# Attention in strips of the tensor array, double-width evictions, and a ring of its own for the residual's input

## What is computed

```python
def xattn(query, key_value, Wq, bq, Wk, bk, Wv, bv, Wo, bo):     # 16 heads of 32
    q, k, v = query @ Wq + bq, key_value @ Wk + bk, key_value @ Wv + bv   # then split into heads
    attn = softmax(clip(einsum('bhqd,bhkd->bhqk', q, k) * 32 ** -0.5, -10000, 10000))
    return einsum('bhqk,bhkd->bqhd', attn, v).reshape(B, Nq, Cq) @ Wo + bo

def ffn(x, emb, w1, w2):                 # 8 experts, each token to its best 2, capacity 1024
    weights = router(x, emb)             # softmax over the two best logits
    # of each expert the first 1024 tokens that chose it
    inter = relu(tokens @ w1[e].T);  out = (inter @ w2[e].T) * gate
    # scattered back by addition

x = x + xattn(layernorm(x), ctx, ...)
x = x + ffn(layernorm(x), ...)
```

## Time and profile before

| what | value |
|---|---|
| time, median of 3 runs | 1538.28 us (1538.25 to 1545.6) |
| time of the profiled execution | 1524.85 us |
| its span, first to last instruction | 1523.1 us |
| mean granted TensorE clock | 0.965 of full speed |
| PE busy | 1411.5 us (93%) |
| DVE busy | 982.1 us (64%) |
| ACT busy | 825.6 us (54%) |
| POOL busy | 857.8 us (56%) |
| DMA | 215.09 MB, 141 GB/s |

### The profile page before, as it was taken

One profiled execution on the slowest core, in us unless ns is written; L12 is line 12 of the kernel. 1 busy time (PEld: TensorE's weight loads), 2 busy tenths in 40 slices (PEclk: granted clock), 3 DMA queues, 4 the chain that ended last, 5 costly groups with the idle time before them and its releaser, 6 DMA issues.

```text
span 1523.1 us, 23892 instructions
## 1 busy us (share of the span) xinstructions
PE 1411.5 (93%) x8807; PEld 875.2 (57%) x8807; DVE 982.1 (64%) x1950; ACT 825.6 (54%) x1472; POOL 857.8 (56%) x907
## 2 busy tenths in 40 slices
PE   6787999989998999999964899999999999999996
PEld 2565777768776777768743644444444444444442
DVE  7895898978877877787766454545454555545430
ACT  4675787668886888768854451504233342425120
POOL 2596788879997899878966414232232414151301
PEclk9898999999999999999976999999999999999998
DMA  6166877568664655746734347465556556474401
GB/s 227 47 154 141 187 200 175 128 143 209 149 145 92 150 122 129 191 102 148 187 93 142 98 129 182 128 171 149 149 164 159 161 127 165 125 196 116 114 14 42
DMA packets 312062, 215.09 MB, mean 141 GB/s; under 512 B 252345, under 2 KB 252729, under 8 KB 311946
## 3 DMA queue, kind: packets, MB, share of 16 engines
q1 hardware_dynamic: 295411, 162.84, 43.6%
q0 software_dynamic: 15360, 50.66, 11.3%
q10 hardware_dynamic: 1175, 0.07, 0.1%
HBM read 105.62 MB, written 50.86 MB: 103 GB/s over the span
## 4 chain that ended last, share of the span: by engine, by line
PE 79%; DVE 5%; SPq 4%; POOL 4%; ACT 3%; issue 2%; DMA 2%; ACTq 1%; DVEq 0%; POOLq 0%
PE ps L1314 22%; PE ps L1335 22%; PE ps L634 9%; PE ps L773 7%; PE ps L752 7%; PE ps L670 5%; SPq L494 3%; PE ps L827 2%; PE ps L601 2%; POOL put L1006 1%; PE ps L796 1%; POOL ph L735 1%; DMA pT<-ph 1%; PE ps L464 1%; DMA wvf<-wv 1%
## 5 line engine op out<-in xcount | busy, mean ns | idle before, releaser
L1314 PE MATMUL ps<-xT,w1s 128*128 128x512 f16 (+1 forms) x1632 | 335.2, 368 | 0.0
L1335 PE MATMUL ps<-w2s,hT 128*128 128x512 f16 x1536 | 332.8, 379 | 0.0
L1320 ACT ACTIVATE hT<-ps 128x512 f16<-128x512 f32 (+1 forms) x136 | 77.8, 572 | 359.7 <-PE ps L1314 359.7
L1314 PEld LDWEIGHTS ps<-xT,w1s 128*128 128x128 f16 x1632 | 160.4, 98 | 172.3
L1335 PEld LDWEIGHTS ps<-w2s,hT 128*128 128x128 f16 x1536 | 150.2, 98 | 181.3
L1345 POOL DMA_INDIRECT out_dram<-ys,idx x64 | 71.7, 1120 | 277.6 <-DVE ys L1340 277.6
L634 PE MATMUL ps<-xnT,wqh 128*128 128x256 f16 x1536 | 189.4, 280 | 9.4 <-DVE xnT L614 7.5
L1322 DVE SCALAR_TENSOR_TENSOR hT<-ps,hT 128x512 f16<-128x512 f32 (+1 forms) x136 | 88.9, 658 | 140.6 <-ACT hT L1320 140.5
L735 POOL TENSOR_TENSOR ph<-sd,ph 128x1232 f16<-128x1232 f32 x64 | 161.9, 2530 | 30.6 <-ACT ph L731 30.5
L634 PEld LDWEIGHTS ps<-xnT,wqh 128*128 128x128 f16 x1536 | 153.6, 101 | 33.1 <-DVE xnT L614 9.0
L752 PE MATMUL ps<-pT,vb 128*128 128x256 f16 (+1 forms) x1248 | 161.5, 278 | 11.6 <-issue 10.3
(11 more groups left out here) (185 smaller groups left out, 2200.3 us busy)
## 6 DMA issues: line engine op xcount, KB each, us to landing
xs<-x SPq DMA_DIRECT2D x64, 256.0 KB, 2.9
xt<-x SPq DMA_DIRECT2D x64, 256.0 KB, 3.1
xrow_dram<-x SPq DMA_DIRECT2D x64, 256.0 KB, 3.3
out_dram<-x SPq DMA_DIRECT2D x64, 256.0 KB, 3.5
stage<-w1T SPq DMA_DIRECT2D x8, 2048.0 KB, 10.1
stage<-w2T SPq DMA_DIRECT2D x8, 2048.0 KB, 8.4
wqf<-wq SPq DMA_DIRECT2D x1, 1024.0 KB, 7.7
wof<-wo SPq DMA_DIRECT2D x1, 1024.0 KB, 11.8
```

Of the source, the lines that this page charges most:

```text
L1314: do("pe", lambda q, k=k, a=a, b=b, i=i, last=last: q.matmul(hb[z][:, 0:wide], w1s[e % 2][:, a, k, ic * P:(ic + 1) * P], xT[:, 4 * b + k, ...
L1335: do("pe", lambda q, k=k, a=a, b=b, i=i, last=last: q.matmul(yb[z][:, :], hT[:, a, k, s * P:(s + 1) * P], w2s[e % 2][:, b, k, :], start=(k ...
```

## The change

Keys and queries of one head share 32 partitions. The change addresses the tensor array by strips.

- `s_mm`: one call per tile. Each head gets a matmul of its own on its 32 rows (row strip j) with 77 columns, 48 per tile; strip j writes bank `bS[j]`, so each bank holds one head of every group. All four banks must be free before a tile's scores, and both maxima wait for all of them.
- The heads' order changes by that, so the value columns (`head_at`) and the output weight's rows (four loads) are permuted.
- `pv_mm`: each head writes its own 32 output partitions (column strip j) with the strip's 32 value columns; a head whose keys lie in two chunks has two pieces: 25 pieces by 3 products, 75 matmuls of 256 columns per pair. Two groups share one bank, 256 columns each; `o_hi` and `o_lo` handle 512 columns, two per pair.
- `part` becomes `partq` (2 x 256) for the queries and `parto` (2 x 512) for the output.
- `xt` is a ring of three, freed by the normalisation. The tile is loaded once more (`load_r`) into `xr`, a ring of five freed by the residual; `add_bo` works on it and waits for the load alone.
- `x1T` has one buffer. Planner's ranks and some costs change.

```diff
-XT = 9
+XT = 3
+RT = 5
...
-    "ln1_stats": -6.54, "rsqrt1": 17.94, "ln1_apply": 18.24, "add_bo": 22.74, "tx": -4.11, "tx_hi": 26.0,
...
+    "ln1_stats": 24.37, "rsqrt1": 19.72, "ln1_apply": 29.94, "add_bo": 34.21, "tx": 7.36, "tx_hi": 37.47,
...
-    "tx_lo": 0.65, "q_mm": 1.4, "q_hi": 0.87, "q_lo": 0.76, "s_mm": 0.42, "s_max": 0.45, "s_sub": 0.9, "s_min": 1.32, "s_exp": 1.32,
+    "tx_lo": 0.65, "q_mm": 1.4, "q_hi": 0.87, "q_lo": 0.76, "s_mm": 0.62, "s_max": 0.45, "s_sub": 0.9, "s_min": 1.32, "s_exp": 1.32,
...
-    "pv_mm": 1.15, "o_hi": 0.78, "o_lo": 0.76, "o_mm": 2.7, "residual": 0.0, "t2": 0.5, "t2_copy": 0.6,
+    "pv_mm": 1.7, "o_hi": 1.2, "o_lo": 1.25, "o_mm": 2.7, "residual": 0.0, "t2": 0.5, "t2_copy": 0.6,
...
+        xr = sb("xr", [P, RT, D], F32)
...
-        part = sb("part", [P, 4, GW], F32)
+        partq = sb("partq", [P, 2, GW], F32)
+        parto = sb("parto", [P, 2, 2 * GW], F32)
...
-        x1T = sb("x1T", [P, 2, 4, P], F32)
+        x1T = sb("x1T", [P, 4, P], F32)
...
         def load_x(t):
             dma("sp", lambda e: e.dma_start(xt[:, t % XT, :], x_t[t]), ("l_x", t), t % XT,
-                after=[("x1", t - XT)] if t >= XT else [])
+                after=[("n1", t - XT)] if t >= XT else [])
+
+        def load_r(t):
+            dma("sp", lambda e: e.dma_start(xr[:, t % RT, :], x_t[t]), ("l_r", t), t % RT,
+                after=[("x1", t - RT)] if t >= RT else [])
...
-        dma("sp", lambda e: e.dma_start(wof[:, :, :], wo.rearrange("(c p) n -> p c n", p=P)), ("l_wo",))
-        for t in range(4, XT):
-            load_x(t)
+        wo_j = wo.rearrange("(j g d) n -> j d g n", j=4, g=4)
+        for j in range(4):
+            dma("sp", lambda e, j=j: e.dma_start(wof[DH * j:DH * (j + 1), :, :], wo_j[j]), ("l_wo", j), 0)
...
         def add_bo(t):
-            src = xt[:, t % XT, :]
-            do("pool", lambda e: e.tensor_tensor(src, src, bos[:, :], ALU.add), after=[("n1", t), ("l_bo",)],
+            src = xr[:, t % RT, :]
+            do("pool", lambda e: e.tensor_tensor(src, src, bos[:, :], ALU.add), after=[("l_r", t), ("l_bo",)],
                mark=("xb", t))
...
+        def s_mm(t):
+
+            G, n = divmod(t, TG)
+            b = t // TPB
+            tokens = slice(n * P, (n + 1) * P)
+            for g in range(4):
+                for i, (a, c) in enumerate(((0, 0), (0, 1), (1, 0))):
+                    for j in range(4):
+                        strip = slice(DH * j, DH * (j + 1))
+                        do("pe", lambda e, g=g, a=a, c=c, i=i, j=j, strip=strip: e.matmul(
+                            bS[j][:, NKV * g:NKV * (g + 1)], qT[strip, G % 2, a, g, tokens],
+                            kbv(b, c)[strip, g, j, :], start=(i == 0), stop=(i == 2), tile_position=(DH * j, 0)),
+                           after=[("qlo", G, g), free["S0"], free["S1"], ("kb0", 3), ("kb1", 3)],
+                           mark=("s", t, g) if i == 2 and j == 3 else None)
+            free["S0"], free["S1"] = ("cl", t, 0), ("cl", t, 1)
...
         def s_max(t, half):
             raw, top8 = ps[:, 1 + 2 * half, 320:328], mx[:, t % 2, 8 * half:8 * half + 8]
             do("dve", lambda e: e.tensor_reduce(four(raw), scores(half), AX_X, ALU.max),
-               after=[("s", t, 2 * half + 1)], mark=("raw", t, half))
+               after=[("s", t, 3)], mark=("raw", t, half))
...
+        def pv_mm(G, half):
+
             b = G * TG // TPB
...
+            n, was = take("A", ("pv", G, half))
+            free[f"A{n}"] = ("of", G, half)
+            for g in (2 * half, 2 * half + 1):
+                cols = slice(GW * (g % 2), GW * (g % 2 + 1))
+                spans = [range(NKV * h // P, (NKV * (h + 1) - 1) // P + 1) for h in range(4 * g, 4 * g + 4)]
+                rounds = [(a, d, r) for r in range(max(len(w) for w in spans)) for a, d in ((0, 0), (0, 1), (1, 0))]
+                todo = [(j, spans[j][r], a, d) for a, d, r in rounds for j in range(4) if r < len(spans[j])]
...
+                    do("pe", lambda e, j=j, k=k, c=c, a=a, d=d, K=K, strip=strip, first=first, last=last, cols=cols:
+                       e.matmul(bA[n][strip, cols], vb[0:K, b, a, k, strip], pT[0:K, G % 2, d, c, :], start=first,
+                                stop=last, tile_position=(0, DH * j)),
...
         def t2_copy(t):
-            do("act", lambda e: e.copy(x1T[:, t % 2, :, :].rearrange("p k n -> p (k n)"), bT[:, :]),
-               after=[("t2", t), back("lg", t, 2)], mark=("x1T", t))
+            do("act", lambda e: e.copy(x1T[:, :, :].rearrange("p k n -> p (k n)"), bT[:, :]),
+               after=[("t2", t), back("lg", t, 1)], mark=("x1T", t))
```

More of the change, by code:

```diff
@@ L637, in q_mm @@
                        after=[("xTl", TG * G + TG - 1), was, ("wq16", "lo")], mark=("q", G, g) if last else None)
-        ring = [0, None, None, None, None]
+        ring = [0, 0, None, None, None, None]
         def halves(key, hi, src, after, bias=None):
-            n = ring[0] % 4
-            copy = part[:, n, :]
-            was = ring[1 + n]
-            ring[0] += 1
-            ring[1 + n] = (key[0] + "lo", *key[1:])
+            kind = 0 if key[0] == "q" else 1
+            n = ring[kind] % 2
+            copy = (partq if kind == 0 else parto)[:, n, :]
+            was = ring[2 + 2 * kind + n]
+            ring[kind] += 1
+            ring[2 + 2 * kind + n] = (key[0] + "lo", *key[1:])
             bank_of["half", key] = copy
@@ L742, in p_T @@
                 ph[:, t % 2].rearrange("p a n -> p (a n)")), ("pT", t), t % 2,
[L743 to L745 removed]
+                after=[("plo", t), ("pz", 1 if t else 0), back("pv", G, 2, 1)])
+        def pv_mm(G, half):
             b = G * TG // TPB
[L747 to L756 removed]
@@ L758, in o_hi @@
-        def o_hi(G, g):
-            n = bank_of["pv", G, g]
-            halves(("o", G, g), oT[:, G % 2, 0, g, :], bA[n][:, 0:GW],
-                   [("pv", G, g), ("wo16", "lo"), back("o", TG * G + TG - 1, 2 * TG)])
-        def o_lo(G, g):
-            low(("o", G, g), oT[:, G % 2, 0, g, :], oT[:, G % 2, 1, g, :])
+            n, was = take("A", ("pv", G, half))
[5 more added lines that the diff above has]
+                todo = [(j, spans[j][r], a, d) for a, d, r in rounds for j in range(4) if r < len(spans[j])]
+                ends = {j: max(n for n, piece in enumerate(todo) if piece[0] == j) for j in range(4)}
+                begins = {j: min(n for n, piece in enumerate(todo) if piece[0] == j) for j in range(4)}
+                for i, (j, c, a, d) in enumerate(todo):
+                    k = PAIRS.index((g, c))
+                    K = min(P, KALL - c * P)
+                    strip = slice(DH * j, DH * (j + 1))
+                    first, last = i == begins[j], i == ends[j]
+                    do("pe", lambda e, j=j, k=k, c=c, a=a, d=d, K=K, strip=strip, first=first, last=last, cols=cols:
+                       e.matmul(bA[n][strip, cols], vb[0:K, b, a, k, strip], pT[0:K, G % 2, d, c, :], start=first,
+                                stop=last, tile_position=(0, DH * j)),
+                       after=[("pT", TG * G + m) for m in range(TG)] + [was, vdm[b]],
+                       mark=("pv", G, half) if g % 2 and i == len(todo) - 1 else None)
@@ L766, in o_mm, with o_both, o_hi, o_lo @@
+        def o_both(G, a, half):
+            return oT[:, G % 2, a, 2 * half:2 * half + 2, :].rearrange("p g n -> p (g n)")
+        def o_hi(G, half):
+            n = bank_of["pv", G, half]
+            halves(("o", G, half), o_both(G, 0, half), bA[n][:, :],
+                   [("pv", G, half), ("wo16", "lo"), back("o", TG * G + TG - 1, 2 * TG)])
+        def o_lo(G, half):
+            low(("o", G, half), o_both(G, 0, half), o_both(G, 1, half))
         def o_mm(t):
@@ L826, in logits @@
             for k in range(4):
[L827 removed]
+                do("pe", lambda e, k=k: e.matmul(bM[:, E * j:E * (j + 1)], x1T[:, k, :], embc[:, k, :],
                                                  start=(k == 0), stop=(k == 3)),
@@ L1134, in xattn_moe @@
         stage("load_x", load_x, [(t,) for t in range(XT, T)], at=list(range(T - XT)))
+        stage("load_r", load_r, per(T), 1.0)
         stage("load_s", load_s, [(t,) for t in range(2, T)], at=list(range(T - 2)))
```

70 lines of the change are left out of this document (24 added, 46 removed).

## The result

The change makes the kernel **slower**: 1549.72 us against 1539.87 us (16 runs each), a ratio of 1.0069 (95% interval 1.0049 to 1.0089). The forecast was 1490 us, 3% faster. In the experiments the same file was run again beside the kernel before on one chip: 1537.59 us against 1525.27, a ratio of 1.0088 (1.0056 to 1.0120).

A forecast was written before the change was run, and what follows sets the result against it. PE was taken as the bound in warm stretches (10.8 us per tile), POOL next; 38 us saved there plus 10 at batch ends and ramp made 48, giving a median of 1490 us, own range 1472 to 1515, overall range 1450 to 1542.

The forecast's parts named there:

- What bounds the kernel now: Attention stage, warm stretches: PE bounds at 10.8 us per tile, POOL second at 10.1, DVE 9.3 and ACT 8.8.
- Scores and P·V: PE's matmuls on strips: scores 1.0 us, 0.6 less per tile; P·V 3.4 us per pair, 0.45 less per tile.
- switches between full array and strips: Rival on PE: eight per two tiles at 0.16 us, 0.65 per tile; part of PE staying the bound, chance 0.14.
- Evictions: P·V results leaving PSUM: ACT from 3.0 to 2.4 us per two tiles, POOL from 10.1 to 10.05 per tile.
- Rings: Buffers xt and xr: ACT's xt wait (8.9 us in 500) and POOL's bias wait (14.6) nearly vanish; SP's wait costs nothing.
- The sum: Attention stage: 38 us saved in warm stretches plus 10 at batch ends and ramp, 48 together, giving a median of 1490.
- The new ranks: Planner's order of every queue: an effect between -10 and +10 us, taken as zero.
- Batch ends: Where 16-tile routing batches end, with the ramp: 23 us lost today, of which 10 was taken as regained.
- Banks locked: Rival, score banks: PE stalls 1.65 us per tile for the subtraction, 1573 us; slower cases 0.13 including 0.04 serial strips.
- The falling clock: Rival on PE: idling lowers the mean clock to 0.9, 9.7 becomes 10.8 us; within PE staying the bound, chance 0.14.
- strips one after another: Rival on PE: strips run wholly serially, P·V 8.2 us a pair, PE 12.6 per tile, +115 us; chance 0.04.
- What would show it: Signs if right: POOL 95% or more and PE near 90% from 340 to 460 us, residuals some 650 us apart.

The follow-up runs named there:

- again: The changed kernel unedited, in its second run, beside the kernel before on one chip: 1537.59 us against 1525.27, ratio 1.0088.
- run 11: Not a label of a run: the text says that POOL's two large softmax lines execute 11 and 10 times in again, 12 and 11 before.

## Why the prediction was wrong

- **What bounds the kernel now.** Right as read: PE full, POOL second, DVE and ACT behind.
- **Scores and P·V.** Right in direction, mis-sized against the change: 0.54 us for 1.0, 2.53 for 3.4. PE's need came to 9.1 us per tile, not 9.7, with the switches between full array and strips in it. The forecast gave those 0.16 us each as a rival; the transposes ahead of scores lost 0.10. The Trainium skill's rule on drains ("TensorEngine Tiling (Array Packing)", Key Properties) agrees with these rows, at that price, and decides nothing.
- **Evictions.** Right. In the second run ACT's two 512-column writes take 0.59 and 0.61 us, POOL's low part of 512 columns 1.16 (1.16 to 1.27 was said).
- **Rings.** Half right. ACT no longer waits for `xt`, nor the bias line for ACT; the bias line waits 11.0 us for `xr` instead. "I cost it at nothing while pT has two buffers and PE 1 us of slack per tile" missed the queue. The text spoke of what stands behind load_r, but asked only how long SP waits, never **how much of SP's own time a tile needs and what else is put there in a lump**. The 75 V transfers stand in no term, though the chain of waits of the kernel before goes through them from 290 to 314 us. With them alone rearranged the changed kernel gains 1.44%.
- **The sum.** This is the step that failed: "from 10.8 to POOL's 10.05 plus 1.5%". It took the busiest engine's work as a tile's length once PE was relieved, and put 38 of its 48 us on the stretches where PE had been full. From 340 to 460 us, such a stretch, POOL's two large softmax lines run 11 and 10 times in *again*, 12 and 11 before, and the residual line 11 times for 12: it is no faster. With four engines between 77% and 86% busy and queues in fixed order, a tile's length is set by waits: the changed kernel needs 9.1 of PE and takes 11.2. "The new ranks reorder every queue, between -10 and +10 us, taken as zero" was the same mistake as a term. Other due times made the same instructions 22 us faster, spreading V (and the new plan that came with it) 27, both 44.
- **Batch ends.** "I take 10 of the 23" had the wrong sign. The three slow stretches deepened from 45 to 33, 44 to 39 and 46 to 36 us of PE in 50.
- **Start and end** were left out and lost 5.1 and 6.9 us. By the chain, what follows the last residual is DVE's statistics and PE's logits and transposes, to 821.5 us, and only then POOL's last tables (825.7 to 832.5); before, those tables started at 803.5 and ended at 816.9. The cause of the late start is open.
- **Rivals.** Banks locked: the wait is there, PE for the subtraction 17.1 us in 500 against 3.0, 0.4 us per tile, under the 1.1 at which it was to decide. The falling clock came (0.93 for 0.98) as a companion of the waits. The forecast gave a slower kernel 0.15, by locked banks or by strips one after another; the sign came from neither but from an order and a queue that none named.
- **What would show it.** POOL at 95% or more from 340 to 460 us failed (93%, and 90% in *again*), and so did residuals some 650 us apart (704). Scores and P·V took less than the 1 and 3.4 us said. That `xnf` no longer waits for DMA held. The listed sign "P·V waiting for pT behind load_r on SP" was nearest to the truth, with V's transfers in place of load_r.

## What to carry to other kernels

When a change takes work off the only full engine, do not give the time to the next engine's busy sum: ask which queue or wait ends last in the slowest stretches. Count the issuing queue as an engine of its own, with each transfer's issue time, and look for lumps of small transfers ahead of anything that the critical engine waits for; moving 75 of them apart was worth 1.4% here and 0.7% in the kernel before. A kernel whose queues are ordered for the old balance has to be ordered anew before a change is judged.

## What the runs showed of the hardware that was not expected

- Strips overlap: 48 matmuls of 77 columns on 32 rows take 0.54 us (the prediction's estimates were 0.39 for full overlap and 1.5 for none), 75 of 256 columns on 32-column strips 2.53 (2.6 and 8.2). Four transposes take 0.53 us ahead of strips and 0.43 ahead of full-array matmuls.
- A plain transfer of a small piece holds SP's queue for 0.65 to 1.04 us (median 0.82 in the second run), longer than a load of 256 KB (medians 0.43 to 0.46, 2.6 at most). A transpose of P holds it for 3.0 us at least, 3.8 in the median and up to 8.9 in that run (5.3 before).
- fp32 logit matmuls of 64 columns cost hardly more than those of 8: the line was busy 46.4 us between 200 and 700 us (347 matmuls), 44.3 with 8 columns (344).
